# Layer 0's compressed attention scores: block sums ahead of the keys, scores as columns of the main score products

## The chip, the core and the metric

The kernel runs on one core of a Trainium2 chip. A core has five engines that run side by side, each through its own list of instructions, in order: TensorE (PE in the profile; its weight loads are PEld), VectorE (DVE), ScalarE (ACT), GpSimd (POOL) and SyncE (SP, which here only starts transfers). They wait for each other by semaphores. The metric is the device time of one execution in microseconds. Before the change it is 2512.39 us, the median of three runs (2508.51 to 2516.61).

## The reference, cut to what matters

The program is a two-layer transformer block over 4 sequences of 512 positions and 512 channels. Each layer has two conditioning scans (a bidirectional recurrence over the positions), an attention and a feed-forward part. The change is in layer 0's attention, which has 16 heads of 128 channels and works on blocks of 64 positions:

```python
q = rope((x @ Wq).reshape(b, n, H, HD)); k = rope((x @ Wk).reshape(b, n, H, HD))
k_cmp = k.reshape(b, nb, BS, H, HD).mean(axis=2)          # nb = 8 blocks of BS = 64
s_cmp = einsum('bnhd,bmhd->bhnm', q, k_cmp) * scale       # compressed scores: 8 per query
p_cmp = softmax(where(idx >= blk_end, s_cmp, -1e30)) * any_block_seen
s_full = einsum('bnhd,bmhd->bhnm', q, k) * scale
p_slc = softmax(where(causal & selected, s_full, -1e30))  # 8 of 8 blocks are selected: causal alone
p_swa = softmax(where(causal & (i - j <= 64), s_full, -1e30))
o = p_cmp @ v_cmp * g_cmp + p_slc @ v * g_slc + p_swa @ v * g_swa
out = o.reshape(b, n, H * HD) @ Wo
```

Since `v_cmp` is a mean of `v` over a block, all three attentions are one product with `v`: the kernel adds the three gated probabilities first.

## The kernel before

Layer 0's attention is the function `layer0_attn`. It goes through 4 batches of 16 heads, in groups of four heads; a head's place in its group is `i`, 0 to 3. A head's queries and keys lie transposed (128 channels by 512 positions) in the two halves of `qk`; its 512 queries are four tiles of 128, `j` = 0 to 3, and tile j needs keys 0 to 128(j+1).

**TensorE**, for head g: the projections of q and k (L830, 24 products of 128x512) and of v (L839, 48 products of 128x128); the output projection of the group before, one quarter at a time (`output`, L880, 12 products), for i = 1 to 3 here and for i = 0 only after the scores; then `values` of head g-1 (ten turnings of probabilities, L861, and the products with v, L869); then `scores` of head g (L847, and L849, which adds the causal mask as a product). A product of two float32 operands runs as two passes, and the profile shows two instructions for it. The scores fill three banks of PSUM, `ps[0..2]`; `BANK_TILES` says which tiles stand in which bank: tile 3, then 2 and 0, then 1. One semaphore step per bank releases VectorE.

**The compressed scores** are `cmp_scores(g - 1)`, called from `project` of the next head after six of its 24 products: four products (eight passes, L821) of a query tile with `ksum`, the eight block sums of the keys, into the bank `pso`, which is free once ScalarE has copied the last head's values out.

**VectorE**, per head: pieces of the conditioning scans that belong to i (`dve_forward`, `dve_backward`, a scan is L238, L244 or L257), `output` (L1012), `sum_keys` (L960), then `softmax`: for each tile a maximum over all scores (L968) and a masked copy of the window with its own maximum (L970); the scaled and masked compressed scores (L975), their maximum (L979) and the subtraction of it (L981); `between()`, which has the next scan inputs wkv_ek and wkv_euk (L217, L223) for i = 1 and 3 and the rope product of the next head's q (L956); the sum of the compressed exps (L985), the reciprocals (L989), the coefficients with the gates (L991), the scaled compressed probabilities (L994); four L998 (one per tile: all scores times coefficient plus block value), the rope product of the next k, and four L1006, which add the window's part. The last of these releases the turning on TensorE.

**ScalarE**, per head: copies of v, the turned probabilities and the head's values; `exps` (L735 and L737 for each tile, then the small compressed exp L740); `swap`, which copies the halves of the next q (L728, L729); in the opening batch a part of the weight split.

**GpSimd** makes the second half of rope (L616, L620) that ends in `qk`, the low halves of the head outputs (L607, semaphore `o_low`), products for the scans (L182, L186, joins L196, L205), and in the opening batch the low half of the float16 weight split (L612).

The order on each engine is written out by hand in its `group` function; nothing is planned at run time.

Of the kernel before, what the change touches and what calls it, by code (L numbers as in the profile page):

```python
# [30 lines left out]
P = 128  # L31
B, T, C = 4, 512, 512
CC = C // P
TT = T // P
# [39 lines left out]
BANK_TILES = ((0, (3,)), (1, (2, 0)), (2, (1,)))  # L74

# [266 lines left out]
def layer0_attn(k):  # L342
# [7 lines left out]
    with ExitStack() as ctx:  # L350
        def sb(n, s, dt=F32):
# [19 lines left out]
        qk = sb("qk", [P, 2, T])  # L371
        ksum = sb("ksum", [P, NBLK])
# [28 lines left out]
            "cmp_ps", "nmax", "sc", "expd", "cmp_step", "cmp_e", "coef", "p_step", "p", "turned", "t_sb", "pv", "of", "o_hi", "o_lo",  # L401
# [6 lines left out]
        def cols(t, j, lo=0, hi=None):  # L408

            bank, c0 = score_columns(j)  # L410
            hi = P * (j + 1) if hi is None else hi
            return t[bank][:, c0 + lo:c0 + hi] if isinstance(t, list) else t[:, bank, c0 + lo:c0 + hi]
# [68 lines left out]
        with nc.Block() as block:  # L481
# [100 lines left out]
            def _(pool):  # L582
# [12 lines left out]
                pool.affine_select(out=cmask[:], in_=cmask[:], compare_op=ALU.is_ge, fill=NEG, base=1 - BLK,  # L595
                                   pattern=[[P, TT], [-BLK, NBLK]], channel_multiplier=1).then_inc(s["const"], 1)

                pool.affine_select(out=seen[:], in_=seen[:], compare_op=ALU.is_ge, fill=0.0, base=1 - BLK,
                                   pattern=[[P, TT]], channel_multiplier=1).then_inc(s["const"], 1)
# [14 lines left out]
                def rope(g, n):  # L614
# [5 lines left out]
                    pool.tensor_tensor(qk[:, n, :], ra[:, n, :], rb[:, n, :], ALU.add).then_inc(s["q_sb"], 1)  # L620
# [45 lines left out]
            def _(act):  # L666
# [64 lines left out]
                def exps(g):  # L731
                    for bank, tiles in BANK_TILES:
                        act.wait_ge(s["nmax"], g * 3 + bank + 1)
                        for j in tiles:
                            act.activation(cols(ps, j), cols(ps, j), ACT.Exp, bias=nmax[:, 0, j:j + 1],  # L735
                                           accum_out=sums[:, 1, j:j + 1]).then_inc(s["expd"], 1)
                            act.activation(wcols(ewn, j), wcols(sw, j), ACT.Exp, bias=nmax[:, 1, j:j + 1],  # L737
                                           scale=-1.0, accum_out=sums[:, 2, j:j + 1]).then_inc(s["expd"], 1)
                    act.wait_ge(s["cmp_step"], g * CMP_STEPS + 2)
                    act.activation(ec[:], sc2[:], ACT.Exp).then_inc(s["cmp_e"], 1)  # L740
# [62 lines left out]
            def _(pe):  # L803
                PARTS = ((0, 0), (0, 1), (1, 0))

                def gates(b):

                    pe.wait_ge(s["y_here"], b * 16 + 16)
                    for t in range(TT):
                        for c in range(CC):  # L810
                            for n, (yp, wp) in enumerate(PARTS):
                                mm = pe.matmul(psg[:, t * 48:t * 48 + 48], y16[:, yp, c, t * P:(t + 1) * P],
# [12 lines left out]
                def project(g, i, ready, scored):  # L825
                    pe.wait_ge(s[f"w_ready{i % 2}"], ready)
                    for n in range(2):
                        for c in range(CC):
# [3 lines left out]
                            if scored and n == 0 and c == 1:  # L832
                                cmp_scores(g - 1)
# [1826 lines left out]
```

## Time and profile before

| what | value |
|---|---|
| median of three runs | 2512.39 us |
| the profiled execution's own time | 2509.32 us |
| its span | 2507.6 us |
| TensorE busy | 2096.8 us, 84% of the span |
| VectorE busy | 1765.7 us, 70% |
| ScalarE busy | 1354.3 us, 54% |
| GpSimd busy | 1102.8 us, 44% |
| mean granted TensorE clock | 0.921 of full speed |

Layer 0's attention fills the first 1356 us, with its first scores at 94 us; the opening batch's heads end at 460.7 us. Busy time is the time in which an engine worked at an instruction, its waits left out; a busy share says little on what sets the time, since the engines hand the work to each other. The time line lists instructions in order, like ones merged: start, duration from the first start to the last end, engine, line, what is written and read, and in brackets the idle time before it with the engine that ended it. The engine records overlap a little, TensorE's above all, where one product's end lies behind the next one's start.

### The profile page before, as it was taken

What the parts mean: (1) busy time and instruction counts of PE and PEld (TensorE: products, weight loads), DVE (VectorE), ACT (ScalarE), POOL (GpSimd) and SP (SyncE); (2) the same over time, 40 slices, a digit from 0 to 9 for tenths busy, and PEclk for the clock granted to TensorE, in tenths of its full rate; (3) what the DMA queues carried; (4) which work ended last, traced back from release to release, by engine and by line L of the source; (5) the groups of instructions that cost most, each with busy time, mean ns of one, the idle gap of its engine ahead of it and who ended that gap; (6) DMA issues with size and microseconds to landing.
All of it is one profiled execution on the core that took longest, in us unless ns stands there. A gap on an engine that the chain in (4) does not pass through costs nothing. (4 is left out here: it accounts for less than half of the span.)

```text
span 2507.6 us, 43574 instructions
## 1 busy us (share of the span) xinstructions
PE 2096.8 (84%) x14585; PEld 1307.7 (52%) x14585; DVE 1765.7 (70%) x3446; ACT 1354.3 (54%) x3223; POOL 1102.8 (44%) x759
## 2 busy tenths in 40 slices
PE   0578888999998999999997649976789898966999
PEld 0355555565555655666664535543556666633444
DVE  7788878788877888886665439854676767644770
ACT  4565656555555555655553513325676766646442
POOL 5565646555655555654443036643322222210440
PEclk9989989999999999999998569986889898978999
DMA  4232223222222221221111874445333333337010
GB/s 165 80 99 79 84 93 107 72 83 67 72 74 86 72 71 61 88 85 58 65 50 61 313 297 137 143 177 177 130 112 114 103 117 116 117 111 246 34 46 21
DMA packets 112588, 268.53 MB, mean 107 GB/s; under 512 B 10800, under 2 KB 40880, under 8 KB 109872
## 3 DMA queue, kind: packets, MB, share of 16 engines
q1 hardware_dynamic: 93312, 217.50, 25.7%
q10 hardware_dynamic: 16560, 40.64, 5.0%
q0 software_dynamic: 2560, 8.39, 0.9%
q8 instruction: 89, 1.46, 0.3%
q14 instruction: 67, 0.55, 0.1%
HBM read 182.60 MB, written 76.55 MB: 103 GB/s over the span
## 5 line engine op out<-in xcount | busy, mean ns | idle before, releaser
L830 PE MATMUL ps_q<-a_y,a_w 128*128 128x512 f16 x1536 | 355.2, 381 | 0.0
L616 POOL TENSOR_TENSOR a_rb<-a_rb,a_rot 128x512 f32<-128x512 f32 x129 | 187.1, 1450 | 307.4 <-ACT a_rb L729 307.4
L830 PEld LDWEIGHTS ps_q<-a_y,a_w 128*128 128x128 f16 x1536 | 149.3, 101 | 162.5 <-issue 3.8
L620 POOL TENSOR_TENSOR a_qk<-a_ra,a_rb 128x512 f32<-128x512 f32 x129 | 204.6, 1586 | 18.9 <-POOL a_rb L616 0.5
L257 DVE TENSOR_TENSOR_SCAN wkv_bwd<-wk_decay,wkv_tail,wkv_fwd 128x512 f32<-128x512 f32 x114 | 197.6, 1756 | 0.1
L880 PE MATMUL ps_g<-a_o,a_wo 128*128 (+1 forms) x768 | 177.8, 381 | 14.1 <-POOL a_o L607 11.6
L869 PE MATMUL ps_o<-a_tt_,a_v 128*128 128x512 f32 (+3 forms) x512 | 176.6, 493 | 11.5 <-ACT a_tt_ L747 9.9
L847 PE MATMUL ps_s<-a_qk 128*128 128x512 f32 (+3 forms) x512 | 173.5, 461 | 13.8 <-POOL a_qk L620 13.8
L839 PEld LDWEIGHTS ps_v<-a_w,a_y 128*128 128x128 f16 x3072 | 176.9, 98 | 15.1
L839 PE MATMUL ps_v<-a_w,a_y 128*128 128x128 f16 x3072 | 182.0, 219 | 0.0
L968 DVE TENSOR_REDUCE a_nmax<-ps_s 128x1 f32<-128x512 f32 (+3 forms) x256 | 124.6, 487 | 74.5 <-PE ps_s L849 67.9
L182 POOL TENSOR_TENSOR wkv_ekv<-wkv_ek,wkv_kt 128x512 f32<-128x512 f32 x57 | 85.6, 1502 | 197.5 <-DVE wkv_ek L217 197.5
L728 ACT ACTIVATE a_rb<-ps_q 64x512 f32<-64x512 f32 x129 | 76.5, 593 | 176.1 <-DVE a_ra L956 174.8
L861 PE MATMUL ps_s<-ident,a_pt 128*128 128x128 f32 x640 | 96.5, 306 | 79.3 <-DVE a_pt L1006 79.3
L1006 DVE SCALAR_TENSOR_TENSOR a_pt<-a_ewn,a_coef,a_pt 128x192 f32<-128x192 f32 (+1 forms) x256 | 155.3, 665 | 0.0
L735 ACT ACTIVATE ps_s<-ps_s,a_nmax 128x512 f32<-128x512 f32 (+3 forms) x256 | 126.6, 495 | 47.7 <-DVE a_nmax L970 45.1
L1881 ACT ACTIVATE a_t<-ps 128x512 f16<-128x512 f32 (+1 forms) x192 | 88.3, 525 | 115.8 <-PE ps L2032 104.9
L747 ACT ACTIVATE a_tt_<-ps_s 128x512 f32<-128x512 f32 (+1 forms) x192 | 88.3, 526 | 99.1 <-PE ps_s L861 98.5
L1874 ACT ACTIVATE a_ef<-ps,a_nmax 128x512 f32<-128x512 f32 (+3 forms) x260 | 133.7, 535 | 11.5 <-DVE a_nmax L2181 10.0
L869 PEld LDWEIGHTS ps_o<-a_tt_,a_v 128*128 128x128 f32 x512 | 93.1, 213 | 84.2 <-ACT a_tt_ L747 42.0
L2500 PE MATMUL psf_h<-f_y,f_w 128*128 128x512 f16 x512 | 113.1, 383 | 26.5 <-DVE f_w L2524 26.5
L861 PEld LDWEIGHTS ps_s<-ident,a_pt 128*128 128x128 f32 x640 | 82.2, 157 | 96.7 <-DVE a_pt L1006 91.9
(271 smaller groups left out, 4941.5 us busy)
## 6 DMA issues: line engine op xcount, KB each, us to landing
a_w<-wqkv_split SPq DMA_DIRECT2D x48, 768.0 KB, 4.6
scratch_numlog<-wkv_nl ACTq DMA_DIRECT2D x40, 512.0 KB, 3.1
wkv_kt<-in_fT ACTq DMA_DIRECT2D x59, 256.0 KB, 2.7
a_wraw<-in_wqkv SPq DMA_DIRECT2D x18, 768.0 KB, 5.4
wqkv_split<-a_w SPq DMA_DIRECT2D x17, 768.0 KB, 6.8
a_stacks<-qk_parts SPq DMA_DIRECT2D x102, 128.0 KB
gate_up<-in_gate_up SPq DMA_DIRECT2D x8, 1408.0 KB, 14.2
a_nlc<-scratch_numlog SPq DMA_DIRECT2D x18, 512.0 KB, 4.5
```

What stands on the lines that cost most here:

```text
L257: dve.tensor_tensor_scan(self.bwd[:, m, ::-1], self.decay(b, n), self.fwd[:, m, ::-1], self.tail[:, m:m + 1], ALU.mult, ALU.add).then_inc( ...
L616: pool.tensor_tensor(rb[:, n, :], rb[:, n, :], rot[:, 2 * n + 1, :], ALU.mult).then_inc(s["roped"], 1)
L620: pool.tensor_tensor(qk[:, n, :], ra[:, n, :], rb[:, n, :], ALU.add).then_inc(s["q_sb"], 1)
L735: act.activation(cols(ps, j), cols(ps, j), ACT.Exp, bias=nmax[:, 0, j:j + 1], accum_out=sums[:, 1, j:j + 1]).then_inc(s["expd"], 1)
L830: mm = pe.matmul(psq[n][:], w16[:, i % 2, wp, n, c, :], y16[:, yp, c, :], start=c + m == 0, stop=c == CC - 1 and m == 2)
L839: mm = pe.matmul(psv[:, t * D0:(t + 1) * D0], y16[:, yp, c, t * P:(t + 1) * P], w16[:, i % 2, wp, 2, c, :], start=c + m == 0, stop=c == CC ...
L847: pe.matmul(cols(ps, j), qk[:, 0, j * P:(j + 1) * P], qk[:, 1, 0:P * (j + 1)], start=True, stop=False)
L861: mm = pe.transpose(ps[bank][:, c0 + (j - m) * P:c0 + (j - m + 1) * P], cols(pt, j, m * P, (m + 1) * P), k.ident[:])
L869: mm = pe.matmul(pso[:, m * P:], v[:, i % 2, m, :], tt_[:, bank, c0:c0 + T - m * P], start=n == 0, stop=n == TT - 1)
L880: mm = pe.matmul(psg[:], wo16[:, wp, bass.ds(c, 1), h, co * P:(co + 1) * P] .rearrange("p a n -> p (a n)"), o_part(og, op, h), start=h + m ...
L1006: dve.scalar_tensor_tensor(out=win(pt, j), in0=wcols(ewn, j), scalar=coef[:, 2, j:j + 1], in1=win(pt, j), op0=ALU.mult, op1=ALU.add).then_ ...
L1874: act.activation(cols(ef[:, i % 2], j), cols(ps[i % 2], j), ACT.Exp, bias=nmax[:, i % 2, j:j + 1], accum_out=sums[:, i % 2, j:j + 1]).then ...
```

## The change

The block sums `ksum` no longer have a tile of their own: keys and sums share the tile `kk`, the eight sums in front of the 512 keys. A score product of tiles 2, 0 and 1 reads from column 0 of `kk` and so writes eight more columns, the compressed scores of that query tile, in front of its scores. Tile 3 fills its bank with 512 columns; its compressed scores are one product of their own, into bank 1. `cmp_scores` and its place in the projection go. The layout of the banks changes (`BANK_TILES0`): tile 3; tile 2 and both tiles' compressed scores; tiles 0 and 1. TensorE waits for the sums ahead of bank 1. VectorE sums the keys ahead of its `condition` and `output` and scales and masks the compressed scores in two operations, one in bank 1's and one in bank 2's step. ScalarE does the small exp ahead of the exps of tiles 0 and 1. The order of the tiles in the small statistics (`sums`, `coef`, gates, masks) becomes 0, 1, 3, 2 (`TILE_SLOT`), and the two masks are cut by two GpSimd operations each at the start, in place of one each.

```diff
+def score_columns0(j):
+    return {3: (0, 0), 2: (1, 2 * NBLK), 0: (2, NBLK), 1: (2, P + 2 * NBLK)}[j]
+BANK_TILES0 = ((0, (3,)), (1, (2,)), (2, (0, 1)))
+TILE_SLOT = (0, 1, 3, 2)
...
-        qk = sb("qk", [P, 2, T])
-        ksum = sb("ksum", [P, NBLK])
+        q = sb("q", [P, T])
+        kk = sb("kk", [P, NBLK + T])
+        ksum = kk[:, 0:NBLK]
+        qk = (q[:], kk[:, NBLK:])
...
 ScalarE, exps(g):
-                    for bank, tiles in BANK_TILES:
+                    for bank, tiles in BANK_TILES0:
                         act.wait_ge(s["nmax"], g * 3 + bank + 1)
+                        if bank == 2:
+                            act.wait_ge(s["cmp_step"], g * CMP_STEPS + 2)
+                            act.activation(ec[:], sc2[:], ACT.Exp).then_inc(s["cmp_e"], 1)
                         for j in tiles:
...
-                    act.wait_ge(s["cmp_step"], g * CMP_STEPS + 2)
-                    act.activation(ec[:], sc2[:], ACT.Exp).then_inc(s["cmp_e"], 1)
...
 TensorE:
-                def cmp_scores(g):
-                    pe.wait_ge(s["ksum"], g + 1)
-                    if not (isinstance(g, int) and g == 0):
-                        pe.wait_ge(s["of"], g)
-                    for j in range(TT):
-                        mm = pe.matmul(pso[:, j * NBLK:(j + 1) * NBLK],
-                                       qk[:, 0, j * P:(j + 1) * P], ksum[:], start=True, stop=True)
-                    mm.then_inc(s["cmp_ps"], 1)
...
-                            if scored and n == 0 and c == 1:
-                                cmp_scores(g - 1)
...
                 def scores(g):
                     pe.wait_ge(s["q_sb"], g * 2 + 2)
-                    for bank, tiles in BANK_TILES:
+                    for bank, tiles in BANK_TILES0:
+                        if bank == 1:
+                            pe.wait_ge(s["ksum"], g + 1)
                         for j in tiles:
-                            pe.matmul(cols(ps, j), qk[:, 0, j * P:(j + 1) * P], qk[:, 1, 0:P * (j + 1)],
+                            lead = NBLK if bank else 0
+                            pe.matmul(cols(ps, j, -lead), q[:, j * P:(j + 1) * P], kk[:, NBLK - lead:NBLK + P * (j + 1)],
                                       start=True, stop=False)
                             mm = pe.matmul(cols(ps, j, P * j), k.ident_b[:], k.causal_b[:],
                                            start=False, stop=True)
+                        if bank == 1:
+                            mm = pe.matmul(ps[1][:, 0:NBLK], q[:, 3 * P:4 * P], ksum, start=True, stop=True)
                         mm.then_inc(s["scores"], 1)
...
 VectorE, softmax:
+                    products = (None, ps[1][:, 0:2 * NBLK].rearrange("p (t m) -> p t m", t=2),
+                                ps[2][:, 0:2 * (P + NBLK)].rearrange("p (t m) -> p t m", t=2)[:, :, 0:NBLK])
...
+                        if bank:
+                            slots = slice(4 - 2 * bank, 6 - 2 * bank)
+                            i = dve.scalar_tensor_tensor(out=sc[:, slots], in0=products[bank], scalar=1.0 / BLK,
+                                                         in1=cmask[:, slots], op0=ALU.mult, op1=ALU.add)
                         i.then_inc(s["nmax"], 1)
-                    dve.wait_ge(s["cmp_ps"], g + 1)
-                    dve.scalar_tensor_tensor(
-                        out=sc[:], in0=pso[:, 0:TT * NBLK].rearrange("p (t m) -> p t m", t=TT),
-                        scalar=1.0 / BLK, in1=cmask[:], op0=ALU.mult, op1=ALU.add).then_inc(s["sc"], 1)
-                    dve.wait_ge(s["sc"], g + 1)
+                    dve.wait_ge(s["nmax"], g * 3 + 3)
                     dve.tensor_reduce(cmax[:], sc[:], AX, ALU.max).then_inc(s["cmp_step"], 1)
...
 VectorE, group:
+                        if i == 3:
+                            for m in range(2):
+                                wkv.dve_backward(dve, u1, b, c * LAYERS + 1, m)
+                        sum_keys(g)
                         if i == 2 and not final(b):
                             dve.wait_ge(wkv.s["num"], u + 1)
                             condition((b + 1) * CC + c, bn, c)
-                        if i == 3:
-                            for m in range(2):
-                                wkv.dve_backward(dve, u1, b, c * LAYERS + 1, m)
...
                         if i and (output_before or not first):
                             output(it - 1, i, b * CC if first else b * CC + CC)
-                        sum_keys(g)
                         softmax(b, g, c * G + i, between)
```

## Rows read from the trace of the kernel before

**Rows 1.** Windows: length, busy us of PE, PEld, DVE, ACT, POOL, clock, DMA share, GB/s.

```profile
94.20:460.70 366.50, 303.92 (x1952) 192.94 (x1952) 292.51 (x559) 220.89 (x499) 214.13 (x131) 0.89 0.28 88
460.70:1068.00 607.30, 569.50 (x4000) 360.11 (x4000) 504.94 (x1125) 348.31 (x933) 345.30 (x232) 0.99 0.23 75
```

**Rows 2.** Groups of instructions by line and form, 0 to 1450 us: busy, mean ns.

```profile
L821 PE MATMUL ps_o<-a_ksum,a_qk 128*128 128x8 f32 x512 | 61.9, 247 | 0.0
...
L847 PE MATMUL ps_s<-a_qk 128*128 128x512 f32 x128 | 68.5, 617 | 13.8 <-POOL a_qk L620 13.8
```

**Rows 3.** Waits, 0 to 1450 us: total, times.

```profile
PEld ps_s L861 <- DVE a_pt L1006: 91.9, 39, 8.0
```

**Rows 4.** Time line of PE, heads i=3 and i=0 of the middle: start, us.

```profile
902.14 1.46 PE L830 MATMUL ps_q<-a_y,a_w 128*128 128x512 f16 x6
...
904.25 4.04 PE L830 MATMUL ps_q<-a_y,a_w 128*128 128x512 f16 x18
...
912.98 2.40 PE L861 MATMUL ps_s<-ident,a_pt 128*128 128x128 f32 x10 [2.01 <-DVE a_pt L1006]
...
917.95 1.02 PE L847 MATMUL ps_s<-a_qk 128*128 128x512 f32 x2
...
921.58 2.76 PE L880 MATMUL ps_g<-a_o,a_wo 128*128 x12 [0.92 <-POOL a_o L607]
```

**Rows 5.** Windows: after the idle time at 912.98.

```profile
912.90:917.90 5.00, 4.92 (x18) 3.83 (x19) 4.87 (x5) 1.85 (x4) 3.15 (x2) 0.66 0.33 135
```

**Rows 6.** Time line of all engines, head i=1 of the middle, S = 705.64.

```profile
705.64 1.02 PE L847 MATMUL ps_s<-a_qk 128*128 128x512 f32 x2
...
709.33 0.35 DVE L970 CUSTOM_DVE_ANT_0 a_sw<-ps_s,a_wmask 128x192 f32<-128x192 f32 x1
...
710.47 0.19 DVE L975 SCALAR_TENSOR_TENSOR a_sc<-ps_o,a_cmask 128x32 f32<-128x32 f32 x1 [0.78 <-PE ps_o L821]
...
711.18 0.43 DVE L217 TENSOR_SCALAR wkv_ek<-wkv_ek_raw 128x512 f32<-128x512 f32 x1
...
711.74 0.22 ACT L740 ACTIVATE a_ec<-a_sc 128x32 f32<-128x32 f32 x1
...
712.96 0.23 DVE L989 RECIPROCAL a_rsum<-a_sums 128x12 f32<-128x12 f32 x1 [0.20 <-DVE a_sums L985]
713.15 1.26 POOL L186 TENSOR_TENSOR wkv_eukv<-wkv_euk,wkv_kt 128x512 f32<-128x512 f32 x1
...
713.33 1.11 DVE L991 TENSOR_TENSOR a_coef<-a_rsum,a_gate 128x12 f32<-128x12 f32 x1
...
714.38 1.26 POOL L616 TENSOR_TENSOR a_rb<-a_rb,a_rot 128x512 f32<-128x512 f32 x1
714.48 1.22 DVE L994 TENSOR_TENSOR a_pc<-a_ec,a_coef 128x32 f32<-128x32 f32 x1
...
724.50 1.13 PE L847 MATMUL ps_s<-a_qk 128*128 128x512 f32 x2 [0.76 <-POOL a_qk L620]
```

**Rows 7.** Time line of DVE and PE, the next head, i=2.

```profile
732.12 0.17 DVE L991 TENSOR_TENSOR a_coef<-a_rsum,a_gate 128x12 f32<-128x12 f32 x1 [0.17 <-DVE a_rsum L989]
...
734.99 1.57 DVE L1006 SCALAR_TENSOR_TENSOR a_pt<-a_ewn,a_coef,a_pt 128x192 f32<-128x192 f32 x4
...
738.40 1.25 PE L861 MATMUL ps_s<-ident,a_pt 128*128 128x128 f32 x10
...
741.96 1.02 PE L847 MATMUL ps_s<-a_qk 128*128 128x512 f32 x2
```

**Rows 8.** Time line, a head of the opening batch.

```profile
307.43 3.10 POOL L612 TENSOR_TENSOR a_w<-a_wraw,a_w 128x1536 f16<-128x1536 f32 x1 [0.59 <-ACT a_w L672]
307.94 5.80 DVE L1006 SCALAR_TENSOR_TENSOR a_pt<-a_ewn,a_coef,a_pt 128x192 f32<-128x192 f32 x4
```

**Rows 9.** Time line of PE and DVE, head i=0, S = 684.60.

```profile
684.60 1.02 PE L847 MATMUL ps_s<-a_qk 128*128 128x512 f32 x2
...
685.55 0.68 DVE L960 TENSOR_REDUCE a_ksum<-a_qk 128x8 f32<-128x512 f32 x1
```

More of the change, by code:

```diff
@@ L408, in cols @@
         def cols(t, j, lo=0, hi=None):
-            bank, c0 = score_columns(j)
+            bank, c0 = score_columns0(j)
             hi = P * (j + 1) if hi is None else hi
@@ L593, in _ @@
                                    pattern=[[-1, 3 * BLK]], channel_multiplier=1).then_inc(s["const"], 1)
[L595 to L599, printed above, removed]
+                for slots, base, step in ((slice(0, 2), 0, P), (slice(2, 4), 3 * P, -P)):
+                    pool.affine_select(out=cmask[:, slots], in_=cmask[:, slots], compare_op=ALU.is_ge, fill=NEG,
+                                       base=base + 1 - BLK, pattern=[[step, 2], [-BLK, NBLK]],
+                                       channel_multiplier=1).then_inc(s["const"], 1)
+                    pool.affine_select(out=seen[:, slots], in_=seen[:, slots], compare_op=ALU.is_ge, fill=0.0,
+                                       base=base + 1 - BLK, pattern=[[step, 2]],
+                                       channel_multiplier=1).then_inc(s["const"], 1)
                 def y_low(c, n):
@@ L619, in rope @@
                     pool.wait_ge(s["roped"], g * 2 + n + 1)
-                    pool.tensor_tensor(qk[:, n, :], ra[:, n, :], rb[:, n, :], ALU.add).then_inc(s["q_sb"], 1)
+                    pool.tensor_tensor(qk[n], ra[:, n, :], rb[:, n, :], ALU.add).then_inc(s["q_sb"], 1)
                 pool.wait_ge(s["wg_hi"], 1)
@@ L894, in group @@
                             gates(b)
-                        project(g, i, 16 * pairs(b, c, i), i or before)
+                        project(g, i, 16 * pairs(b, c, i))
                         if i and before:
@@ L941, in _ @@
                     condition(c, 0, c)
-                dve.wait_ge(s["const"], 8)
+                dve.wait_ge(s["const"], 10)
                 dve.wait_ge(s["rot"], 16)
@@ L959, in sum_keys @@
                     dve.wait_ge(s["q_sb"], g * 2 + 2)
-                    dve.tensor_reduce(ksum[:], qk[:, 1, :].rearrange("p (m n) -> p m n", n=BLK), AX,
+                    dve.tensor_reduce(ksum, qk[1].rearrange("p (m n) -> p m n", n=BLK), AX,
                                       ALU.add).then_inc(s["ksum"], 1)
@@ L964, in softmax @@
                     c = g * CMP_STEPS
-                    for bank, tiles in BANK_TILES:
+                    products = (None, ps[1][:, 0:2 * NBLK].rearrange("p (t m) -> p t m", t=2),
+                                ps[2][:, 0:2 * (P + NBLK)].rearrange("p (t m) -> p t m", t=2)[:, :, 0:NBLK])
+                    for bank, tiles in BANK_TILES0:
                         dve.wait_ge(s["scores"], g * 3 + bank + 1)
@@ L996, in softmax @@
                     dve.wait_ge(s["coef"], g + 1)
-                    for n, j in enumerate((3, 2, 1, 0)):
+                    for j in (3, 2, 1, 0):
+                        n = TILE_SLOT[j]
                         dve.scalar_tensor_tensor(
                             out=cols(pt, j).rearrange("p (m n) -> p m n", n=BLK),
-                            in0=cols(ps, j).rearrange("p (m n) -> p m n", n=BLK), scalar=coef[:, 1, j:j + 1],
-                            in1=pc[:, j, 0:2 * (j + 1)].unsqueeze(2).to_broadcast([P, 2 * (j + 1), BLK]),
+                            in0=cols(ps, j).rearrange("p (m n) -> p m n", n=BLK), scalar=coef[:, 1, n:n + 1],
+                            in1=pc[:, n, 0:2 * (j + 1)].unsqueeze(2).to_broadcast([P, 2 * (j + 1), BLK]),
                             op0=ALU.mult, op1=ALU.add).then_inc(s["p_step"], 1)
@@ L1005, in softmax @@
                         dve.wait_ge(s["p_step"], g * TT + n + 1)
-                        dve.scalar_tensor_tensor(out=win(pt, j), in0=wcols(ewn, j), scalar=coef[:, 2, j:j + 1],
+                        dve.scalar_tensor_tensor(out=win(pt, j), in0=wcols(ewn, j), scalar=coef[:, 2, TILE_SLOT[j]:TILE_SLOT[j] + 1],
                                                  in1=win(pt, j), op0=ALU.mult, op1=ALU.add).then_inc(s["p"], 1)
```

13 lines of the change are left out of this document (7 added, 6 removed).

## Prediction

> **What bounds the kernel now.** I read the totals of stretches first. From the first score products to the end of layer 0's attention (94 to 1356 us) TensorE is busy 303.9 of 366.5 us in the opening batch and 569.5 of 607.3 in the middle two; VectorE 293 and 505 [rows 1]. So TensorE is nearly full in the later heads and waits in the first 16. The waits say on whom: its weight loads for the turning of the probabilities waited 91.9 us, 39 times, for VectorE's last window product (L1006) [rows 3]. The time line, head by head, tells which of the two chains closes a head. I count from S, the first score product of a head. TensorE's chain: scores, projection (24+48 products), output (12), turning. VectorE's chain ("p" below): maxima, ScalarE's exps, sums, coefficients, four L998, rope, four L1006.
>
> Four kinds of heads repeat, in the middle batches nearly to the hundredth:
> - i=2: the last L1006 is over at 734.99+1.57 = 736.56, the turning starts at 738.40 [rows 7]: TensorE's chain decides, with 1.84 us to spare. i=0 looks the same (slack 1.84 in all 8).
> - i=1: both end within a tenth of each other; then the next head's scores wait 0.76 us for GpSimd's roped keys [rows 6], which follow VectorE's chain.
> - i=3: no output products, TensorE is idle 2.01 us before the turning [rows 4]: p decides.
>
> **What goes.** The compressed scores stand inside the q projection. Six projection products started at 902.14; eighteen take 4.04 us [rows 4], so one starts every (4.04-0.38)/17 = 0.215 us and the seventh would have started at 903.43. It started at 904.25. The eight passes of L821 cost **0.82 us** of TensorE a head, 52 us in 64 heads (their busy time is 61.9 [rows 2], part of it overlapped).
>
> **What comes on TensorE.** Eight more columns on three products of two passes: at most 8 x 617/512 ns [rows 2] x 6 = 0.06 us. One 128x8 product stays and stands in bank 1: a quarter of 0.82 = 0.21; its lower bound is 0 (hidden like the causal products), its upper one its two passes alone, 2 x 0.247 = 0.49 [rows 2]. I take 0.25, as it stands between other kinds of products. Net: 0.82-0.04-0.25 = **0.53 us a head** (0.27 to 0.82).
>
> **VectorE and ScalarE, worked out for the i=1 head at S = 705.64 [rows 6].**  Before: maxima until 709.68, then a wait of 0.78 us, the scaled compressed scores at 710.47, wkv_ek at 711.18, the reciprocal at 712.96. The wait goes. Two small operations replace one: +0.2 us, one of them before bank 1's release. Bank 1's products end about 0.25 later; VectorE would have been free 0.07 before that. So: bank 2's maxima end 709.84, its scaled scores 709.99, cmax and the subtraction (0.22 us apart, as before) end 710.43, wkv_ek starts 710.51: 0.67 earlier. ScalarE now does the small exp ahead of tiles 0 and 1. It is done with tile 2 at 710.12 and waits for the subtraction: exp at 710.47, tiles 0 and 1 after it (0.73 and 0.98 us by the old spacing) until 712.40. Before, the exps ended at 711.83. So ScalarE is held back **0.57 us**; but VectorE reached the reciprocal only at 712.96, behind wkv_ek, wkv_euk and the rope. These move up 0.67, so the reciprocal now starts at 712.44, released by ScalarE: 0.52 earlier.
>
> The coefficients took 1.11 us and the product after them 1.22 us, where the first takes 0.17 in the next head [rows 7]. They end 0.03 and 0.06 us after GpSimd's two products (713.15+1.26, 714.38+1.26) [rows 6]: each sat out one GpSimd operation. GpSimd's chain starts from wkv_ek and moves up 0.67, so the second one ends at about 714.97 and L998 starts at 715.04 instead of 715.73.
>
> The Trainium skill, "SBUF — State Buffer", its list under the two sides of SBUF, has this as a rule: a VectorE operation with two SBUF inputs and a GpSimd operation share a port pair as an exclusive lock, and whoever starts first holds it for the whole instruction. The trace agrees. By that rule p moves up 0.69 here, by unchanged durations 0.52: some 2 us over the 11 heads of this kind. From it follows that a tenth of a microsecond in a start can flip who waits, in either direction.
>
> **By kind of head.**
> - i=1 (12 heads of batches 1 to 3): p and the keys move 0.7, TensorE 0.53; since keys' roping closes the next start, 0.7 for 11, 0.5 for one: **8.2**. If it is TensorE alone: 6.4.
> - i=2 (12): TensorE 0.53, p perhaps 0.1 to 0.5 later (roping, condition and ScalarE's hold), inside the 1.84 of slack: **6.4**. The key sums move ahead of condition and output; the same operations, other order.
> - i=0 (12): the output products wait for GpSimd's o_low, at 921.58, 0.92 us idle [rows 4]. The 0.29 us added to the scores falls into this idle time, so the full 0.82 is won: 9.8. Against it: bank 1 now waits for the key sums, which started 0.95 us after S in a head such as that at 684.60 [rows 9], and end 0.7 after bank 0; the same idle time covers most of it; at the three batch starts they are later still. I take 1.5 off: **8.3**.
> - i=3 (12): p decides. In the middle batches wkv_ek moves up 0.67 and wkv_euk behind it, p follows by 0.6: 8 x 0.6. In the last batch nothing stands between the subtraction and the rope, the reciprocal is released by ScalarE's later end: 0.2, 0.3, 0.3, 0. Together **5.6**.
> - Opening batch: p decides in all 16, and four L1006 take 5.80 us with GpSimd's 3.10 us weight split among them [rows 8]; the split hangs on ScalarE, which gains 0.1 to 0.3. I take 0.2 for 13 and 0.8 for the three with an output before the projection: **5.0**.
> - Start-up: two more small mask operations on GpSimd, under 0.5 us; taken as nothing.
>
> Sum 8.2+6.4+8.3+5.6+5.0 = 33.5 us.
>
> **Off again.** After the idle 2.01 us at 912.98 the granted clock fell: its mean over the next 5 us is 0.66 [rows 5], between 2.4 and 1.2 GHz. From turning to scores took 917.95-912.98 = 4.97 us [rows 4], where the head at 738.40 took 3.56 [rows 7]: 1.4 us a drop; four of the heads with 2 us or more of idle time in the middle have it. A head where TensorE gets faster than p idles longer. I take two or three more drops, 3.5 us. Net **30 us**.
>
> The profiled execution took 2509.3 us (span 2507.6 and 1.7 around it), 3.1 under the median of 2512.4. 2509.3-30 = 2479.3 in its own terms; by the median, **2482**.
>
> **Rivals.**
> 1. TensorE's share only: p does not move where it decides (each tenth gained is lost again to a GpSimd operation or to ScalarE's order), and TensorE gains 0.53 only where it decides, 24 heads of i=0 and 2 plus half the i=1. For: ScalarE's hold is exactly there; in the last batch's i=3 heads it leaves nearly nothing. Against: GpSimd's own chain moves up as well. 24 x 0.6 + 6 x 0.5 = 17: 2495.
> 2. More than forecast: the locks fall well. In i=1 and i=3 heads the second small product slips in between two GpSimd operations and saves 1.2 us more, in some 15 heads of all batches: 18 us. For: ScalarE's later end delays the rope's GpSimd half, which opens that gap. Against: by my times it misses by 0.1 us. 2464 to 2470.
> 3. Slower: ScalarE's hold takes the place of the wait. Place: tiles 0 and 1 behind the small exp. Price: 0.57 us in each head where p decides (39 waits of rows 3), and, if the coefficient then meets one more GpSimd operation of 1.27 us, that too. It decides as soon as the exps end more than 0.5 us after my 712.40-S = 6.76, since the reciprocal stood at 7.32. 39 x 0.57 + 20 x 1.27 = 48 lost, 25 to 30 won elsewhere: about 2530. By the rows VectorE was the later one, so this is unlikely.
> 4. The key sums: bank 1 waits for VectorE in many heads. In i=1 and 3 they start 0.53 before S and now still earlier, in i=2 about when q and k are there, 0.33 us before bank 1 needs their end. If a third of the heads lost 0.7 us, 15 us: 2497.
>
> **Chances.** Forecast 0.5 (own range 2474 to 2490), rival 1 0.18, rival 2 0.13, rival 4 0.12, rival 3 0.07. This kernel's runs spread over 8 us, so 0.3% (7.5 us) is what can be told from no change. Rivals 1 and 4 mostly stay faster than that bound (2505); 0.08 of them and a little of the rest fall within. Faster 0.85, same 0.09, slower 0.06. The range that leaves out 0.2: 2466 to 2500.
>
> **What would show it.** L821 is gone; the 24 projection products run without a break of 0.82 us. VectorE's wait of 0.78 us ahead of the scaled scores is gone. In i=1 heads the reciprocal stands at about S+6.8, waiting for ScalarE, and the small exp waits a few tenths for the subtraction. The heads' periods shrink by 0.8, 0.7, 0.5 and 0.6 (i = 0 to 3, middle batches). TensorE waits for a_ksum only in i=0 heads. It is wrong if turning still waits for L1006 as long as before plus 0.5 in i=1, or if the drops of the clock double.

## The result

The changed kernel takes 2485.6 us (median of four, 2477.1 to 2486.7) against 2513.6; the ratio is 0.9891, 95% interval 0.9863 to 0.9918. The medians are 28 us apart. Measured a second time, the ratio was 0.9913 (0.9882 to 0.9944). So the change makes the kernel faster by 1.1% and 0.9%, by these ratios 22 to 27 us, beyond the 0.3% that can be told from no change. The forecast was 2482 us, that is 30 us less, in a range of 2466 to 2500.

The page of the changed kernel, its span and busy times:

```profile
span 2484.8 us, 42776 instructions
...
PE 2066.0 (83%) x14201; PEld 1266.8 (51%) x14201; DVE 1775.8 (71%) x3510; ACT 1355.0 (55%) x3223; POOL 1107.2 (45%) x761
```

Windows over the same three stretches as before, start of the first scores to the next batch's (length, then busy us of PE, PEld, DVE, ACT, POOL, granted clock, DMA share, GB/s); the last one ends with the attention:

```profile
96.10:457.60 361.50, 295.99 (x1857) 181.45 (x1857) 291.17 (x573) 221.10 (x499) 217.44 (x131) 0.88 0.29 90
457.60:1047.20 589.60, 555.44 (x3809) 339.88 (x3809) 509.95 (x1157) 348.32 (x933) 345.75 (x232) 0.98 0.23 77
1047.20:1330.00 282.80, 263.61 (x1773) 162.08 (x1773) 215.16 (x544) 156.61 (x436) 136.46 (x96) 0.98 0.20 66
```

The first two answer to [rows 1]. The opening batch's heads went from 366.5 to 361.5 us, the middle two batches' from 607.3 to 589.6. In the last batch the 15 periods from its first to its last score start went from 273.0 to 269.9 us. The first scores start at 96.1 where they started at 94.2, and all behind the last score start takes 1167.7 where it took 1166.6. The five differences, +1.9, -5.0, -17.7, -3.1 and +1.1, make the -22.8 us between the two spans. In the changed kernel profiled a second time the three stages took 363.5, 587.2 and 271.4 us and all behind the last score start 1173.4. So the attention from its first to its last score start went from 1246.8 us to 1221.0 and 1222.1, while the part behind it, the last head's end and all that follows the attention, lies between 1158 and 1173 us in the twelve profiled executions. That stretch is the better measure of small differences, and it is used below as "the attention stretch". VectorE's busy time rose by 10 us and ScalarE's stayed; TensorE's fell by 31.

TensorE's time line over the scores of an i=1 head of the middle, S = 698.39:

```profile
698.39 1.02 PE L858 MATMUL ps_s<-a_kk,a_q 128*128 128x512 f32 x2
...
699.30 0.88 PE L858 MATMUL ps_s<-a_kk,a_q 128*128 128x392 f32 x2
700.02 0.22 PE L860 MATMUL ps_s<-causal_b,ident_b 128*128 128x128 bf16 x1
700.08 0.34 PE L863 MATMUL ps_s<-a_kk,a_q 128*128 128x8 f32 x2
700.27 0.48 PE L858 MATMUL ps_s<-a_kk,a_q 128*128 128x136 f32 x2
700.59 0.22 PE L860 MATMUL ps_s<-causal_b,ident_b 128*128 128x128 bf16 x1
700.64 0.66 PE L858 MATMUL ps_s<-a_kk,a_q 128*128 128x264 f32 x2
...
701.20 5.34 PE L840 MATMUL ps_q<-a_y,a_w 128*128 128x512 f16 x24
```

The break in the projection is gone: all 24 products run without one from 701.20. The scores' last causal product ends at S+2.97 where it ended at S+2.71: **0.26 us** came on, 0.29 was forecast. The next score product starts 0.19 us behind the start of the 128x8 product ahead of it.

The same head on the other engines, to be read against [rows 6]:

```profile
703.12 0.43 DVE L229 TENSOR_SCALAR wkv_ek<-wkv_ek_raw 128x512 f32<-128x512 f32 x1
...
704.38 0.45 ACT L757 ACTIVATE a_ewn<-a_sw,a_nmax 128x192 f32<-128x192 f32 x1
...
704.97 0.23 DVE L1003 RECIPROCAL a_rsum<-a_sums 128x12 f32<-128x12 f32 x1 [0.20 <-ACT a_ewn L757]
705.09 1.26 POOL L198 TENSOR_TENSOR wkv_eukv<-wkv_euk,wkv_kt 128x512 f32<-128x512 f32 x1
705.35 1.03 DVE L1005 TENSOR_TENSOR a_coef<-a_rsum,a_gate 128x12 f32<-128x12 f32 x1
...
706.31 1.27 POOL L632 TENSOR_TENSOR a_rb<-a_rb,a_rot 128x512 f32<-128x512 f32 x1
...
706.41 1.22 DVE L1008 TENSOR_TENSOR a_pc<-a_ec,a_coef 128x32 f32<-128x32 f32 x1
707.67 1.93 DVE L1013 SCALAR_TENSOR_TENSOR a_pt<-ps_s,a_coef,a_pc 128x512 f32<-128x512 f32 x4
```

wkv_ek starts at S+4.73, where it was at 5.54; the reciprocal at S+6.58 (7.32), within 0.15 us of ScalarE's last exp, which ends at 704.38+0.45 = 704.83 and whose sum is read out by 704.92; forecast were 4.87 and 6.80. ScalarE's exps end at S+6.53 where they ended at S+6.20: it is held back 0.33 us, where the prediction had 0.57. The coefficients end at 706.38, 0.03 behind GpSimd's product (705.09+1.26), and the next product at 707.63, 0.05 behind the second one (706.31+1.27): VectorE is blocked twice, as before. L998 starts at S+9.28, forecast 9.40, before 10.10.

The waits over 0 to 1450 us (total, times, longest), against [rows 3]:

```profile
PEld ps_s L874 <- DVE a_pt L1021: 85.5, 47, 9.1
...
ACT a_ec L752 <- DVE a_sc L995: 26.4, 64, 1.5
...
PEld ps_s L858 <- DVE a_kk L972: 11.6, 17, 2.0
...
DVE a_rsum L1003 <- ACT a_ewn L757: 11.0, 34, 1.1
```

TensorE's loads waited 85.5 us for p in place of 91.9, 47 times in place of 39. The two new waits are there: the small exp waits 0.4 us in each head, and the weight loads for bank 1 waited 11.6 us in all for the key sums. The score products themselves waited for the sums six times, 0.6 to 1.5 us each, always in an i=0 head, as forecast.

### The profile page after: what moved, and what is told of

It reads as the page before. It is cut to its first block and busy times, and to the rows that moved or that the text cites. A ratio compares the mean times of both kernels' runs of the same rounds, so it can differ in the third digit from the quotient of the medians.

```text
span 2484.8 us, 42776 instructions
## 1 busy us (share of the span) xinstructions
PE 2066.0 (83%) x14201; PEld 1266.8 (51%) x14201; DVE 1775.8 (71%) x3510; ACT 1355.0 (55%) x3223; POOL 1107.2 (45%) x761
## 5 line engine op out<-in xcount | busy, mean ns | idle before, releaser
L840 PE MATMUL ps_q<-a_y,a_w 128*128 128x512 f16 x1536 | 345.0, 381 | 0.0
L858 PE MATMUL ps_s<-a_kk,a_q 128*128 128x512 f32 (+3 forms) x512 | 193.8, 487 | 27.3 <-POOL a_kk L636 22.6
L269 DVE TENSOR_TENSOR_SCAN wkv_bwd<-wk_decay,wkv_tail,wkv_fwd 128x512 f32<-128x512 f32 x114 | 188.3, 1674 | 0.1
L1021 DVE SCALAR_TENSOR_TENSOR a_pt<-a_ewn,a_coef,a_pt 128x192 f32<-128x192 f32 (+1 forms) x256 | 168.2, 715 | 0.0
L882 PEld LDWEIGHTS ps_o<-a_tt_,a_v 128*128 128x128 f32 x512 | 94.2, 216 | 86.2 <-ACT a_tt_ L765 41.5
L968 DVE TENSOR_TENSOR a_ra<-ps_q,a_rot 128x512 f32<-128x512 f32 x130 | 89.1, 686 | 64.8 <-PE ps_q L840 64.3
L198 POOL TENSOR_TENSOR wkv_eukv<-wkv_euk,wkv_kt 128x512 f32<-128x512 f32 x57 | 79.5, 1394 | 118.6 <-DVE wkv_euk L235 118.6
```

The costliest lines, as they stand in the source:

```text
L269: dve.tensor_tensor_scan(self.bwd[:, m, ::-1], self.decay(b, n), self.fwd[:, m, ::-1], self.tail[:, m:m + 1], ALU.mult, ALU.add).then_inc( ...
L840: mm = pe.matmul(psq[n][:], w16[:, i % 2, wp, n, c, :], y16[:, yp, c, :], start=c + m == 0, stop=c == CC - 1 and m == 2)
L858: pe.matmul(cols(ps, j, -lead), q[:, j * P:(j + 1) * P], kk[:, NBLK - lead:NBLK + P * (j + 1)], start=True, stop=False)
L882: mm = pe.matmul(pso[:, m * P:], v[:, i % 2, m, :], tt_[:, bank, c0:c0 + T - m * P], start=n == 0, stop=n == TT - 1)
L1021: dve.scalar_tensor_tensor(out=win(pt, j), in0=wcols(ewn, j), scalar=coef[:, 2, TILE_SLOT[j]:TILE_SLOT[j] + 1], in1=win(pt, j), op0=ALU.mu ...
```

## The experiments

Ratios are to the kernel before, run on the same chip beside the edited one. "Periods" are differences of the first score products' starts of neighbouring heads, means over the eight heads of a kind in the middle batches.

**Own products.** Merging taken back, placement kept.

```diff
-                            lead = NBLK if bank else 0
+                            lead = 0
...
+                            if bank:
+                                mm = pe.matmul(cols(ps, j, -NBLK, 0), q[:, j * P:(j + 1) * P], ksum, start=True, stop=True)
```

> The changed kernel, but tiles 2, 0 and 1 have compressed products of their own (128x8, two passes each) beside the score products, which lose their eight columns; the place in the scores, the layout and all other orders stay. It splits the change into moving and merging. My theory (TensorE pays about 0.25 us for each such product, and it delays the banks): scores longer by 0.6 us; free in i=0 (idle ahead of the output), 0.5 in i=2, 0.3 to 0.5 in i=1 and 3 through the later maxima, the like in the opening batch: about 2505, so merging is some three quarters of the gain. Rival (the gain comes from the place alone, since VectorE no longer waits and the small products hide behind the score products' weight loads): within 4 us of 2486.

Measured: 2506.3 us, ratio 0.9997 (0.9979 to 1.0016). The attention stretch is 1247.1 us, against 1246.8 in the kernel before. The scores' place alone, with VectorE's wait gone, is worth nothing; three pairs of passes more in the scores take the whole gain back. The period of i=2 is 17.51 us against 16.91, of i=1 18.63 against 18.04: 0.2 us a product. I had expected merging to be some three quarters of the gain; it is all of it that can be told.

**Twice.** Tile 3's own product made two times.

```diff
-                            mm = pe.matmul(ps[1][:, 0:NBLK], q[:, 3 * P:4 * P], ksum, start=True, stop=True)
+                            for _ in range(2):
+                                mm = pe.matmul(ps[1][:, 0:NBLK], q[:, 3 * P:4 * P], ksum, start=True, stop=True)
```

> The changed kernel, with tile 3's own compressed product (128x8, two passes) made twice. It prices one such product: my 0.25 us a head. Theory A: 0.2 to 0.25 us of TensorE, free in i=0 (idle ahead of the output), paid in i=2, and by the later bank 1 in part of i=1 and 3: 5 to 9 us slower, ratio 0.991 to 0.993. Rival (hidden behind the neighbours' weight loads): 0.989.

Measured: 2491.0 us, ratio 0.9939 (0.9913 to 0.9966). The time line of PE in a head of the middle:

```profile
707.33 0.22 PE L860 MATMUL ps_s<-causal_b,ident_b 128*128 128x128 bf16 x1
707.38 0.56 PE L864 MATMUL ps_s<-a_kk,a_q 128*128 128x8 f32 x4
707.80 0.48 PE L858 MATMUL ps_s<-a_kk,a_q 128*128 128x136 f32 x2
```

From the 128x8 products' first start to that of the next score product it is 0.42 us where it was 0.19 above: 0.23 for the pair of passes, and the i=2 period is 17.14 against 16.91, the same 0.23. The product is not hidden. The ratio is a little above the 0.991 to 0.993 that I had expected, and its interval overlaps that of the changed kernel; it is the rows that settle the price.

**No compressed products at all.** The kernel before, which here leaves them out: VectorE's L975 reads 32 of bank 2's scores in their place, inside that bank's step.

```diff
-                            if scored and n == 0 and c == 1:
-                                cmp_scores(g - 1)
...
+                        if bank == 2:
+                            i = dve.scalar_tensor_tensor(
+                                out=sc[:], in0=ps[2][:, 0:TT * NBLK].rearrange("p (t m) -> p t m", t=TT),
+                                scalar=1.0 / BLK, in1=cmask[:], op0=ALU.mult, op1=ALU.add)
                         i.then_inc(s["nmax"], 1)
-                    dve.wait_ge(s["cmp_ps"], g + 1)
...
-                    dve.wait_ge(s["sc"], g + 1)
+                    dve.wait_ge(s["nmax"], g * 3 + 3)
```

> The kernel before, with the compressed score products left out altogether: L975 reads 32 scores of bank 2 in their place, ahead of that bank's release. It has VectorE's wait and TensorE's 0.82 us away and nothing added, neither columns nor the waits for the key sums, and ScalarE's order is the old one. My theory: 0.82 us in each head where TensorE decides and 0.5 to 0.8 where p does: 40 us, 2473; the changed kernel got about 28, the rest being the added 0.26 us a head, the wait for the key sums at the batch starts and the flips. Rival (the added parts cost nothing): 2486.

Measured: 2461.8 us, ratio 0.9819 (0.9788 to 0.9850), 45 us of gain, and 45.0 in the attention stretch; 40 were expected. The i=2 period is 16.65 where it was 17.46: 0.81 for the break that I had put at 0.82. This is about what a rearrangement of these products alone could have won; the change won a little over half of it.

**Key sums late.** The sums behind `condition` and `output` again.

```diff
-                        sum_keys(g)
                         if i == 2 and not final(b):
...
+                        sum_keys(g)
                         softmax(b, g, c * G + i, between)
```

> The changed kernel, with VectorE's key sums back behind condition and output, where the kernel before has them. It prices the wait of bank 1 for the sums. Theory A: in the i=2 heads of the first three batches the sums then end 1.9 us after S, bank 1 waits 1 us for them and TensorE's chain decides there: 9 heads x 1 us, in i=1 and i=3 they are still in time: 7 to 12 us slower than the changed kernel, ratio 0.992 to 0.994. Rival (TensorE's wait is covered by what VectorE does late anyway, the maxima): ratio 0.989.

Measured: 2484.3 us, ratio 0.9929 (0.9902 to 0.9956); the interval overlaps that of the changed kernel, so the total doesn't decide. The periods show a price in one kind of head: i=2 takes 17.81 in place of 16.91, i=1 18.04 as in the changed kernel. The row of such an i=2 head in the time line:

```profile
714.86 0.93 PE L858 MATMUL ps_s<-a_kk,a_q 128*128 128x392 f32 x2 [0.69 <-DVE a_kk L972]
```

Bank 1 waits for the sums there, at 0.9 us a head. But the opening batch took 357.7 us here, where it took 361.5 and 363.5 in the changed kernel, and the attention stretch is 1222.6 against 1221.0 and 1222.1. That moving the sums ahead made the whole kernel faster is not shown.

**Small exp last** on ScalarE, as in the kernel before.

```diff
-                        if bank == 2:
-                            act.wait_ge(s["cmp_step"], g * CMP_STEPS + 2)
-                            act.activation(ec[:], sc2[:], ACT.Exp).then_inc(s["cmp_e"], 1)
...
+                    act.wait_ge(s["cmp_step"], g * CMP_STEPS + 2)
+                    act.activation(ec[:], sc2[:], ACT.Exp).then_inc(s["cmp_e"], 1)
```

> The changed kernel, with ScalarE's small exp back behind the exps of all tiles. The prediction had ScalarE held back by it (tiles 0 and 1 wait some tenths for VectorE's subtraction) and the reciprocal released by ScalarE's end. Theory A (either order ends at about the same place, as VectorE then has to sum the small exps after the last exp): the tiles' exps end 0.2 to 0.3 us earlier, the small exp ends at S+6.4, and the reciprocal moves from S+6.58 to about S+6.8: 0 to 6 us slower than the changed kernel's ratio of 0.989, so 0.989 to 0.992. Rival (ScalarE's hold costs p in each head where p decides): 0.3 us in 39 heads, 8 to 12 us faster, ratio 0.985.

Measured: 2481.5 us, ratio 0.9897 (0.9871 to 0.9923): no difference that can be told. The reciprocal stands at S+6.58 in an i=1 head in both, so ScalarE's order costs p nothing directly there. I had expected it 0.2 later; but VectorE sums the small exps at S+6.21 in both, and with the small exp last the reciprocal follows that sum. The last batch did change: it takes 264.6 us in place of 269.9 and, the second time, 271.4. The opening one takes 364.5 in place of 361.5 and 363.5, which is too little to tell. The section on the prediction comes back to that.

**Keys behind p.** GpSimd waits for the head's last window product before it ropes the next keys, in the changed kernel and in the kernel before.

```diff
                         g = b * H0 + c * G + i
+                        if not (isinstance(g, int) and g == 0):
+                            pool.wait_ge(s["p"], g * TT)
                         rope(g, 1)
```

> The changed kernel, with one wait more: GpSimd starts the two rope products of the next keys only when VectorE's four window products (p) of the head before are done. Theory A (VectorE's operations with two SBUF inputs and GpSimd's products sit each other out; in the changed kernel the window products now meet GpSimd's products and so p does not come earlier in many heads): the four window products fall back to 1.3 to 1.6 us outside the weight split, TensorE's wait for p falls in the opening batch (by 1.3 to 2.5 us in each of about 10 heads) and in the i=3 heads of the last batch (1.2 us in 3), the keys are still ready in time; 2486 goes to 2450 to 2470. Theory B (p is set by ScalarE's exps and the amount of VectorE's work; GpSimd does not matter): the new wait can only delay the keys, 2486 to 2510.

> The kernel before, with the same added wait of GpSimd for p. Theory A: the opening batch gains as in the changed kernel, since its window products sat out GpSimd's key products too, but the last batch gains nothing (its window products took 1.58 us, one block of 0.25): 2513 to 2485-2500, a gain smaller than in the changed kernel by about 3 to 8 us. Theory B: no gain, 2513 to 2525.

Measured: the changed kernel 2454.5 us, ratio 0.9789 (0.9746 to 0.9832); the kernel before 2491.2 us, ratio 0.9943 (0.9922 to 0.9963). An added wait makes the kernel faster, by 1.0 to 1.2% and 0.6%. The opening batch falls by 20 us in both (361.5 to 341.6, and 366.5 to 346.6); the last batch falls by 6.0 us in the changed kernel and by 1.0 in the one before. The attention stretches fall by 25.2 and 20.7 us, 4.5 apart, inside the 3 to 8 that I expected. The window products came down less far than the 1.3 to 1.6 us that I expected: in the last batch's i=3 heads from 2.81 to 1.81, in most i=1 heads of the opening batch, where the weight split is still among them, from 6.1 to 4.0.

**Weight split behind the keys**, added to that, again in both.

```diff
                         rope(g, 1)
+                        if opening(b) and not (isinstance(g, int) and g == 0):
+                            split(g + 1, (i + 1) % 2)
...
                         rope(g + 1, 0)
-                        if opening(b):
-                            split(g + 2, i % 2)
...
-                run(pool, group, lambda: o_low(B * H0 - 1, (B * CC - 1) % 2, G - 1))
+                run(pool, group, lambda: o_low(B * H0 - 1, (B * CC - 1) % 2, G - 1),
+                    lambda: split(H0 + 1, 1))
```

> The kernel with GpSimd's wait for p (2454 us, ratio 0.979), and in the opening batch GpSimd's 3.1 us weight split moved from before to behind the two key products of the next head. Theory A (VectorE's window products sit out the split): they fall from 4 to 5 us to 1.3 to 1.6, p comes 3 us earlier in 14 heads, the keys with it, and the split now runs beside scans and scores; the projection needs its result only 3 us after the scores' start, so up to 1 us may be lost there and the scans sit it out in part: 1.5 us won a head, 2454 to about 2435, ratio 0.971. Rival (the split only moves the blocking on to the scans, and the keys' sums and the maxima come late): 2450 to 2465.

> The kernel before with both GpSimd edits (keys behind p, weight split behind the keys). Against the changed kernel with the same two edits (2436 us, ratio 0.9718) it gives what the change is worth where the window products hardly meet GpSimd. Theory A (the change earns 0.53 us of TensorE in i=2 and about 0.8 in i=0, 1 and 3, and in the plain kernels the collisions took some of it back, in the last batch above all): the gap is 33 to 40 us against 28 for the plain kernels, so this one is at 0.985 to 0.988 of the kernel before. Rival (the collisions take from both alike): a gap of 28, ratio 0.983.

Measured: the changed kernel 2436.3 us, ratio **0.9718** (0.9685 to 0.9751), the fastest of all; the kernel before 2473.4 us, ratio 0.9861 (0.9828 to 0.9895). In an opening head of the changed kernel, without either edit, the four window products, the key products and the split stood as follows:

```profile
308.84 3.10 POOL L628 TENSOR_TENSOR a_w<-a_wraw,a_w 128x1536 f16<-128x1536 f32 x1 [0.90 <-ACT a_w L688]
309.03 6.11 DVE L1021 SCALAR_TENSOR_TENSOR a_pt<-a_ewn,a_coef,a_pt 128x192 f32<-128x192 f32 x4
...
311.89 1.38 POOL L632 TENSOR_TENSOR a_rb<-a_rb,a_rot 128x512 f32<-128x512 f32 x1
...
313.41 1.26 POOL L636 TENSOR_TENSOR a_kk<-a_ra,a_rb 128x512 f32<-128x512 f32 x1
```

6.11 us for four products that take 1.33 alone. With both edits, another opening head:

```profile
283.69 1.33 DVE L1024 SCALAR_TENSOR_TENSOR a_pt<-a_ewn,a_coef,a_pt 128x192 f32<-128x192 f32 x4
...
285.18 2.64 POOL L632 TENSOR_TENSOR a_rb<-a_rb,a_rot 128x512 f32<-128x512 f32 x1 [2.60 <-DVE a_pt L1024]
...
287.96 1.99 POOL L636 TENSOR_TENSOR a_kk<-a_ra,a_rb 128x512 f32<-128x512 f32 x1
...
289.92 3.10 POOL L628 TENSOR_TENSOR a_w<-a_wraw,a_w 128x1536 f16<-128x1536 f32 x1
```

They take 1.33, and the split runs beside the next head's scores. The opening batch is at 324.9 us where it was at 361.5.

The two ratios give 0.9718/0.9861 = 0.9855: with most of these collisions away the change is worth 36 us (the medians are 37 apart), and in the attention stretch 36.0, by batch 7.7, 20.0 and 8.2. In the plain kernels the stretch gave 25.8 and 24.7. The ratios by themselves don't separate the two cases: each is known to some 0.3 to 0.5%. Of the 7.7 us of the opening batch 4.1 stand in its last head alone. With keys behind p only, the two kernels differ by 36.7 us by their medians and by 30.2 in the stretch.

**The changed kernel again.**

> The changed kernel as it is, once more, on the same chip as its neighbour here, so that the gap of the plain kernels is known more closely: ratio 0.987 to 0.991, 2482 to 2488 us where the kernel before takes 2508 to 2513. A rival is only that the first figure lay off by its spread: a ratio outside 0.986 to 0.992.

Measured: 2486.0 us, ratio 0.9913 (0.9882 to 0.9944), just outside the narrow band I gave, inside the one that the rival needed left, and inside the first measurement's interval. The plain kernels' gap is 22 to 27 us by the two ratios, 28 and 19 by the medians.

## Why the prediction was right, and where its sum was off

The mechanism came out as forecast, and the forecast case, not a rival, holds.

- The break of 0.82 us: 0.81 by the kernel without the products. Right.
- What came on TensorE, 0.25+0.04: 0.26 in the scores, 0.23 of it the 128x8 pair.
- Kinds of heads in the middle, the commonest periods of those without drops of the clock: i=0 21.04 to 20.24 (0.80, forecast 0.82), i=1 18.86 to 18.05 (0.81, forecast 0.7), i=2 17.46 to 16.91 (0.55, forecast 0.53), i=3 17.00 to 16.17 (0.83, forecast 0.6). The middle batches gave 17.7 us, and 20.1 in the changed kernel run again; my terms for them make 20.3 before clock drops.
- The mean of the i=0 heads did not move in the first profile (20.72 to 20.71), since head 16, the first of the second batch, took 24.47 us in place of 20.05: the wait for the key sums, and the granted clock at its lower level for 6.8 us from 460.1. In the kernel run again the clock stayed up there, the head took 21.17 and the mean was 20.09. My term for more drops had them behind i=3 heads, not at a batch start.
- The opening batch, 5.0 us: forecast 5.0. Its inside was not as I had it (single heads became up to 4.0 us shorter and up to 2.3 longer), and the kernel run again gave 3.0, so I count the sum as luck.
- The wait for the key sums at a batch start. The first score product of bank 1 in head 16:

```profile
460.20 1.02 PE L858 MATMUL ps_s<-a_kk,a_q 128*128 128x392 f32 x1 [1.46 <-DVE a_kk L972]
```

The wait of 1.46 us is the longest of the six. Most of the i=0 ones lie in the idle time ahead of the output, as forecast: heads with one (28, 44) and one without (36) have the same period, 20.23 and 20.24.

**The failing term is the last batch**: 8.3 us forecast by the kinds, 3.1 measured, and 1.6 in the kernel run again. The step was the i=3 term, "the reciprocal is released by ScalarE's later end: 0.2, 0.3, 0.3", and behind it that p follows the reciprocal. In head 55 the reciprocal was earlier by more than that (S+6.58 for 7.13), L998 by 0.54, and p came *later*, S+12.66 for 11.96. The time line of the kernel before in head 55 (S = 1196.3), GpSimd's second product of the next q, the four window products, GpSimd's first product of the next k, the turning:

```profile
1205.90 1.27 POOL L620 TENSOR_TENSOR a_qk<-a_ra,a_rb 128x512 f32<-128x512 f32 x1
...
1206.73 1.58 DVE L1006 SCALAR_TENSOR_TENSOR a_pt<-a_ewn,a_coef,a_pt 128x192 f32<-128x192 f32 x4
...
1208.12 1.32 POOL L616 TENSOR_TENSOR a_rb<-a_rb,a_rot 128x512 f32<-128x512 f32 x1 [0.95 <-ACT a_rb L729]
...
1208.37 1.31 PE L861 MATMUL ps_s<-ident,a_pt 128*128 128x128 f32 x10 [0.65 <-DVE a_pt L1006]
```

and of the changed kernel (S = 1174.0):

```profile
1183.27 1.27 POOL L636 TENSOR_TENSOR a_q<-a_ra,a_rb 128x512 f32<-128x512 f32 x1
...
1183.87 2.81 DVE L1021 SCALAR_TENSOR_TENSOR a_pt<-a_ewn,a_coef,a_pt 128x192 f32<-128x192 f32 x4
...
1185.26 1.27 POOL L632 TENSOR_TENSOR a_rb<-a_rb,a_rot 128x512 f32<-128x512 f32 x1 [0.72 <-ACT a_rb L745]
...
1186.74 2.04 PE L874 MATMUL ps_s<-ident,a_pt 128*128 128x128 f32 x10 [1.88 <-DVE a_pt L1021]
```

Before, the window products began 0.44 us before GpSimd's product of q ended; p cost 1.58 us. Counted from S, they moved up by 0.54 us and GpSimd's product only by 0.31, so now they begin 0.67 before it ends. That also pushes them into the reach of the key products, which start at 1185.26, and the last of them sits that one out: 2.81 us. TensorE idles 1.88 us in place of 0.65, and from 1187.2 the granted clock is at the lower of its two levels, 1.2 GHz, for 3.4 us (the turning takes 2.04 for 1.31 us). Two of the three i=3 periods of this batch have such a drop, where before none had. Their mean went up from 15.97 to 17.34, and to 17.83 in the kernel run again. With the wait for p on GpSimd, same head (window products, turning, key product):

```profile
1162.95 1.81 DVE L1023 SCALAR_TENSOR_TENSOR a_pt<-a_ewn,a_coef,a_pt 128x192 f32<-128x192 f32 x4
...
1164.82 1.31 PE L876 MATMUL ps_s<-ident,a_pt 128*128 128x128 f32 x10 [0.89 <-DVE a_pt L1023]
1164.93 1.27 POOL L632 TENSOR_TENSOR a_rb<-a_rb,a_rot 128x512 f32<-128x512 f32 x1 [1.31 <-DVE a_pt L1023]
```

1.81 us, the key product comes behind them, the idle time is 0.89, and the i=3 period is 15.34. That kernel's last batch is 9.1 us below that of the kernel before, and 8.1 below that of the kernel before with the same wait, where the terms say 8.3. So the lost 5 to 6 us are the collisions and the clock drops behind them, shown by the one edit that removes them.

The small exp's place decided the same thing from the other side. In the kernel with the small exp last, head 55 (S = 1175.9):

```profile
1184.88 1.27 POOL L636 TENSOR_TENSOR a_q<-a_ra,a_rb 128x512 f32<-128x512 f32 x1
...
1185.71 1.57 DVE L1020 SCALAR_TENSOR_TENSOR a_pt<-a_ewn,a_coef,a_pt 128x192 f32<-128x192 f32 x4
...
1187.10 1.32 POOL L632 TENSOR_TENSOR a_rb<-a_rb,a_rot 128x512 f32<-128x512 f32 x1 [0.95 <-ACT a_rb L745]
```

The last of the tiles' exps ends 0.56 us earlier there, and the small one behind it still 0.44 earlier. GpSimd's q product ends at S+10.29 in place of S+10.52, and these 0.23 us are enough for the fourth window product to get in ahead of the key product: 1.57 us in place of 2.81. So the hold of ScalarE, which the prediction had priced at the reciprocal alone, cost its time here, through GpSimd: the i=3 period of this batch is 15.42 us in that kernel, against 17.34.

The rule that I leaned on is from the Trainium skill, "SBUF — State Buffer", section "SBUF: two separate sides": a VectorE operation with two SBUF inputs and a GpSimd operation that reads SBUF hold a port pair in turn, each for its whole length. These rows agree with it (2.81 us for four products that take 1.33 alone, with the key product of 1.27 us among them). I used it for the two small products and, outside the opening batch, did not carry it on to the four window products, which have two SBUF inputs as well. In the i=2 heads they take 2.86 us now for 1.60, and p comes 1.1 us later by S, where I had 0.1 to 0.5; the slack of 1.84 covers that. In i=3 I gave them no term.

**Start-up**: taken as nothing, the first scores came 1.9 us later. The gate product of the kernel before:

```profile
89.62 1.26 DVE L950 TENSOR_TENSOR a_gate<-a_gate,a_seen 128x64 f32<-128x64 f32 x1
```

and of the changed kernel, with GpSimd's next two products:

```profile
90.05 0.22 DVE L962 TENSOR_TENSOR a_gate<-a_gate,a_seen 128x64 f32<-128x64 f32 x1
...
90.33 2.13 POOL L636 TENSOR_TENSOR a_q<-a_ra,a_rb 128x512 f32<-128x512 f32 x1 [0.51 <-POOL a_rb L632]
92.43 2.17 POOL L632 TENSOR_TENSOR a_rb<-a_rb,a_rot 128x512 f32<-128x512 f32 x1
```

TensorE's first projection happened to end 0.43 us later, VectorE's gate product got in ahead of GpSimd (0.22 for 1.26 us), the scans behind it too, and GpSimd's two products took 2.13 and 2.17 us in place of 1.27 and 1.26: the first keys were late. Why the projection ended 0.43 later was not tried. In the changed kernel run again the first scores start at 96.0 as well; in all eight kernels with the change they start at 95.8 to 97.1, in the four without it at 94.2 to 95.2.

**Clock drops**: I took two or three more over the middle. Time at the lower level rose from 81.9 to 88.7 us in the opening batch's stretch, from 17.1 to 23.9 in the middle's, from 10.2 to 17.1 in the last one's (in the kernel run again 92.2, 17.1 and 20.5). So it rose by a fifth in all and did not double, which was my sign of being wrong. The total has the forecast direction, but not the place: the middle's rise was not there the second time, and the idle time ahead of i=3 turnings in the middle did not grow (2.01 to 1.74), it was the last batch's that did. My 3.5 us for all of it was probably too little; head 16 alone took 3.3 us more with its drop than without.

## What to carry to other kernels

Where two float32 products share their weights and their columns fit one bank, put the small one's columns into the large one: here a 128x8 product cost 0.23 us of TensorE's stream as its own instruction and some hundredths as eight more columns. Where VectorE and GpSimd take turns, a kernel has no fixed price per operation: list each VectorE operation with two SBUF inputs on the chain that matters, lay GpSimd's operations beside it, and check after each shift which one starts first. If the order of the two is left to a race of tenths, fix it with a semaphore so that the operation on the critical chain goes first: that one wait, and the move of the weight split, gave 50 us here, twice what the change itself did.

## What was not expected of the hardware

- An added wait made both kernels faster: 2486 to 2454 us, and 2508 to 2491.
- Eight passes of 128x8 in the middle of a stream of 128x512 products cost 0.81 us, as much as nearly four of these at 0.215.
- In head 55 the tiles' exps ending 0.56 us earlier on ScalarE brought GpSimd's product 0.23 us earlier, and the four window products took 1.24 us less.
